# The value bias of a head attention, moved from VectorE's eviction into the matmul bank

## The reference, cut to what matters

```python
def _L1_xattn_ref(query, key, value, Wq, bq, Wk, bk, Wv, bv, Wo, bo):
    q = (query @ Wq.T + bq).reshape(b, s, N_HEADS, D_K)
    k = (key @ Wk.T + bk).reshape(b, s, N_HEADS, D_K)
    v = (value @ Wv.T + bv).reshape(b, s, N_HEADS, D_K)
    scores = jnp.einsum('bshd,bsgd->bshg', q, k) * inv_sqrt_dk
    attn = jax.nn.softmax(scores, axis=-1)
    out = jnp.einsum('bshg,bsgd->bshd', attn, v)
```

## Time and profile before

| what | value |
|---|---|
| median of 3 runs | 584.02 us (583.33 to 591.06) |
| the profiled execution's own time | 586.47 us |
| its span, first to last instruction | 584.7 us |
| mean granted TensorE clock | 0.954 of full |
| TensorE matmuls busy | 515.5 us (88%) |
| VectorE busy | 425.0 us (73%) |
| ScalarE busy | 331.8 us (57%) |
| GpSimd busy | 199.0 us (34%) |

### The profile page before, as it was taken

One profiled execution on the slowest core, in us unless ns is written; L12 is line 12 of the kernel. 1 busy time (PEld: TensorE's weight loads), 2 busy tenths in 40 slices (PEclk: granted clock), 3 DMA queues, 4 the chain that ended last, 5 costly groups with the idle time before them and its releaser, 6 DMA issues.

```text
span 584.7 us, 13038 instructions
## 1 busy us (share of the span) xinstructions
PE 515.5 (88%) x4832; PEld 321.4 (55%) x4842; DVE 425.0 (73%) x1232; ACT 331.8 (57%) x825; POOL 199.0 (34%) x309
## 2 busy tenths in 40 slices
PE   3887888999999999977488997998989989999995
PEld 2532444544455576756344556776667867655543
DVE  7878567254666667588998768753788557798996
ACT  1764435755768879655267573566566644353441
POOL 6940000024365545341345520000224221434774
PEclk9955889999999999999699999999998989999998
DMA  8700000000300000001324833000000000301101
GB/s 291 307 1 4 2 3 4 2 1 0 145 2 1 1 2 3 2 1 34 169 84 135 179 86 101 3 4 2 2 3 3 3 2 2 145 0 67 80 1 36
DMA packets 25889, 27.93 MB, mean 48 GB/s; under 512 B 18249, under 2 KB 22866, under 8 KB 24930
## 3 DMA queue, kind: packets, MB, share of 16 engines
q1 hardware_dynamic: 25826, 27.10, 14.4%
HBM read 22.14 MB, written 4.75 MB: 46 GB/s over the span
## 4 chain that ended last, share of the span: by engine, by line
PE 59%; DVE 19%; issue 8%; ACT 5%; SPq 3%; DMA 2%; POOL 2%; POOLq 0%; DVEq 0%; ACTq 0%
PE B_banks L312 4%; PE A_banks L312 4%; PE A_banks L2108 2%; PE A_banks L248 2%; PE A_banks L1014 2%; PE A_banks L1027 2%; DVE B_moe_h L2075 2%; SPq L276 2%; PE B_banks L248 2%; PE A_banks L1874 1%; DVE A_l0a_nmax L340 1%; PE B_banks L982 1%; PE A_banks L1884 1%; PE B_banks L1035 1%; PE A_banks L1035 1%
## 5 line engine op out<-in xcount | busy, mean ns | idle before, releaser
L2108 PE MATMUL A_banks<-A_moe_xT,w_moe_rows 128*128 128x512 f32 x72 | 36.0, 617 | 1.3 <-DVE A_moe_h L2075 1.3
L832 POOL TENSOR_TENSOR A_l0x_prob<-A_l0x_prob,A_l0x_inverted_sums 128x256 f32<-128x256 f32 (+1 forms) x32 | 25.9, 831 | 28.5 <-DVE A_l0x_inverted_sums L947 28.5
L2108 PE MATMUL B_banks<-B_moe_xT,w_moe_rows 128*128 128x512 f32 x72 | 34.4, 598 | 1.2 <-DVE B_moe_h L2075 1.1
L832 POOL TENSOR_TENSOR B_l0x_prob<-B_l0x_prob,B_l0x_inverted_sums 128x256 f32<-128x256 f32 (+1 forms) x32 | 25.9, 831 | 27.6 <-DVE B_l0x_inverted_sums L947 27.6
L160 POOL TENSOR_TENSOR A_l0a_rstd<-A_l0a_ve,w_const_rows 128x4 f32<-128x4 f32 x2 | 2.0, 1016 | 87.8 <-DVE A_l0a_ve L156 87.8
L379 ACT ACTIVATE A_l0a_expT<-A_banks 128x512 f32<-128x512 f32 x32 | 18.3, 603 | 18.6 <-PE A_banks L327 18.3
L849 ACT ACTIVATE B_l0x_prob<-B_l0x_prob,B_l0x_nmax 128x128 f32<-128x128 f32 x64 | 28.2, 446 | 0.9 <-DVE B_l0x_nmax L929 0.9
L849 ACT ACTIVATE A_l0x_prob<-A_l0x_prob,A_l0x_nmax 128x128 f32<-128x128 f32 x64 | 28.2, 447 | 0.0
L340 DVE TENSOR_REDUCE A_l0a_nmax<-A_banks 128x2 f32<-128x512 f32 x32 | 21.7, 687 | 8.0 <-PE A_banks L248 7.7
L379 ACT ACTIVATE B_l0a_expT<-B_banks 128x512 f32<-128x512 f32 x32 | 18.4, 600 | 15.9 <-PE B_banks L327 15.9
L340 DVE TENSOR_REDUCE B_l0a_nmax<-B_banks 128x2 f32<-128x512 f32 x32 | 21.9, 688 | 7.3 <-PE B_banks L248 7.3
(11 more groups left out here) (602 smaller groups left out, 1598.6 us busy)
## 6 DMA issues: line engine op xcount, KB each, us to landing
w_toeplitz_rows<-in_toeplitz_rows SPq DMA_DIRECT2D x1, 3072.0 KB, 13.1
w_moe_rows<-in_moe_rows SPq DMA_DIRECT2D x1, 2304.0 KB, 8.6
w_l1x_rows<-in_l1x_rows SPq DMA_DIRECT2D x1, 2048.0 KB, 8.4
A_l1x_values<-A_l1a_v_tokens SPq DMA_DIRECT2D x4, 512.0 KB, 2.6
A_l1x_v_groups<-A_l1x_values SPq DMA_DIRECT2D x16, 128.0 KB, 3.3
B_l1x_values<-B_l1a_v_tokens SPq DMA_DIRECT2D x4, 512.0 KB, 3.4
B_l1x_v_groups<-B_l1x_values SPq DMA_DIRECT2D x16, 128.0 KB, 3.3
w_l0x_vo_rows<-in_l0x_vo_rows SPq DMA_DIRECT2D x1, 1024.0 KB, 13.7
```

The lines of the kernel that those rows point to most:

```text
L832: ins = pool.tensor_tensor(pair, pair, bcast(rz[:, g % 2, i, :], 2, n), ALU.mult)
L2108: pe.matmul(hidden_bank(k)[:, :], w["moe_w3" if which else "moe_w1"][:, ORDER[i], part, :], xT[:], start=True, stop=True).then_inc(s_h.sem, 1)
```

## The change

The value bias is split once into three bfloat16 parts whose sum is the fp32 bias. GpSimd makes them, in five pieces of the program W: two casts and two subtractions of 1024 columns over 128 partitions, a memset, two copies of 32 partitions, and three memsets of one row. They lie where the spread bias lay; partitions 0 to 31 hold the high part, 32 to 63 the middle one, 64 to 95 the low one. `bias_rows` is a 96 x 128 matrix with ones in rows 0, 32 and 64. A values job becomes two products into the same bank: `bias_rows` by the parts (bfloat16, 96 rows, 512 columns), then the fp32 product as before. VectorE's sixteen additions are gone; ScalarE's `context_values` copies the bank to `vt`. TensorE waits for the parts before each lane's first job, and program W has VectorE and ScalarE wait for them before they write the buffers that GpSimd uses as scratch (`r` and `vT`). `TURNS` is new for all five engines; the GpSimd table has its five W turns right after both lanes' last piece of `rel_attention`'s preparation (L518).

```diff
--- before.py
+++ after.py
@@ -1421,6 +1421,13 @@
                 ins = act.activation(heads_kT[:, :, h], job_bank(m)[:, j * S:(j + 1) * S], ACT.Identity, bias=w["l1x_bk"][:, h:h + 1])
             ins.then_inc(s_key.sem, 1)
 
+        def context_values(m):
+            t, half = divmod(jobs[m][1], 2)
+            act.wait_ge(*s_pr(m + 1))
+            if t >= SB:
+                act.wait_ge(*s_vs(16 * (t - SB + 1)))
+            act.activation(vt[:, t % SB, half * 512:(half + 1) * 512], job_bank(m)[:, :], ACT.Copy).then_inc(s_val.sem, 1)
+
         def values(t):
             act.wait_ge(*s_rest(t + 1))
             act.activation(vals[:, t, :, 0:DV], bank[2 + t % 2][:, NQK:W].rearrange("p (h d) -> p h d", h=HK), ACT.Copy).then_inc(s_v.sem, 1)
@@ -1433,11 +1440,14 @@
             ins.then_inc(s_stk.sem, 1)
 
         def all_keys():
-            for m in range(1, JOBS, 2):
+            for m in range(JOBS):
                 yield job_time(m) + 1.0
                 if m == 1:
                     w.loaded(act, "l1x")
-                keys(m)
+                if m % 2:
+                    keys(m)
+                else:
+                    context_values(m)
 
         def all_values():
             yield 5.5
@@ -1474,14 +1484,6 @@
     def vector(dve):
         link = Chain(dve, lane)
 
-        def values(m):
-            t, half = divmod(jobs[m][1], 2)
-            dve.wait_ge(*s_pr(m + 1))
-            if t >= SB:
-                dve.wait_ge(*s_vs(16 * (t - SB + 1)))
-            dve.tensor_tensor(vt[:, t % SB, half * 512:(half + 1) * 512], job_bank(m)[:, :],
-                              w["l1x_bv"][:, half * 512:(half + 1) * 512], ALU.add).then_inc(s_val.sem, 1)
-
         def split(t, due):
             dve.wait_ge(*s_qkv(t + 1))
             if t >= 2:
@@ -1494,13 +1496,6 @@
             link.wait()
             dve.tensor_tensor(sr[:, t % 2, :], qk, hi, ALU.subtract).then_inc(s_rest.sem, 1)
 
-        def all_values():
-            for m in range(0, JOBS, 2):
-                yield job_time(m) + 1.0
-                if m == 0:
-                    w.loaded(dve, "l1x")
-                values(m)
-
         def all_splits():
             for t in range(TT):
                 yield 8.0 + 3.5 * t
@@ -1510,7 +1505,7 @@
         yield from norm.vector_stats(dve, link, x)
         yield
         norm.vector_apply(dve, xn, x, s_xn)
-        yield from interleaved([all_values(), all_splits()])
+        yield from all_splits()
         yield 26.0
         dve.wait_ge(*s_kz(2))
         dve.wait_ge(*s_stT(5))
@@ -1567,7 +1562,9 @@
                 wait_job(pe, m - 2)
             if kind == "v":
                 t, half = divmod(i, 2)
-                ins = pe.matmul(out[:, :], cT[:, t * P:(t + 1) * P], w["l1x_v"][:, half * 512:(half + 1) * 512], start=True, stop=True)
+                columns = slice(half * 512, (half + 1) * 512)
+                pe.matmul(out[:, :], w["bias_rows"], w["l1x_bv_parts"][:, columns], start=True, stop=False)
+                ins = pe.matmul(out[:, :], cT[:, t * P:(t + 1) * P], w["l1x_v"][:, columns], start=False, stop=True)
             else:
                 for j in range(2):
                     for half in range(2):
@@ -1581,6 +1578,7 @@
                 yield job_time(m)
                 if m == 0:
                     w.loaded(pe, "l1x")
+                    pe.wait_ge(*w["bias_parts"])
                 product(m)
 
         def all_projections():
@@ -2166,6 +2164,9 @@
     s_vTp, s_vT, s_vo = (st.own_sem(n) for n in ("v_transposed", "vT_ready", "product_ready"))
     st.chain = [lane.ctx.enter_context(lane.nc.semaphore("weights_chain")), 0]
     s_levels = w["levels"][0]
+    s_bv = w["bias_parts"][0]
+    high, mid = (vT[:].rearrange("p c d -> p (c d)").bitcast(BF16)[:, i * 1024:(i + 1) * 1024] for i in range(2))
+    rest = r[:].rearrange("p i d -> p (i d)")
 
     def sync(sp):
         yield 0.0
@@ -2206,6 +2207,7 @@
         link.add(dve.reciprocal(scale[:], mean[:]))
         yield
         link.wait()
+        dve.wait_ge(*w["bias_parts"])
         for i in range(2):
             link.add(dve.tensor_scalar(r[:, i, :], raw[:, i, :], scale[:, i:i + 1], MAGIC, ALU.mult, ALU.add))
             yield
@@ -2237,6 +2239,8 @@
     def scalar(act):
         for i in range(2):
             yield 61.0
+            if i == 0:
+                act.wait_ge(*w["bias_parts"])
             act.wait_ge(*s_vTp(i + 1))
             act.activation(vT[:, 4 * i:4 * i + 4, :], bank[0][:, :].rearrange("p (c d) -> p c d", c=4), ACT.Copy).then_inc(s_vT.sem, 1)
         yield 65.0
@@ -2244,7 +2248,27 @@
         act.activation(w["l0x_vo"][:], bank[0][:, 0:D], ACT.Copy, scale=1.0 / S).then_inc(s_levels, 1)
 
     def gpsimd(pool):
-        yield from ()
+
+        bias, parts, rows = w["l1x_bv"], w["l1x_bv_all_parts"], w["bias_all_rows"]
+        yield 50.0
+        w.loaded(pool, "l1x_rest")
+        pool.tensor_copy(high, bias).then_inc(s_bv, 1)
+        yield
+        pool.wait_ge(s_bv, 1)
+        pool.tensor_tensor(rest, bias, high, ALU.subtract).then_inc(s_bv, 1)
+        yield
+        pool.wait_ge(s_bv, 2)
+        pool.tensor_copy(mid, rest).then_inc(s_bv, 1)
+        yield
+        pool.wait_ge(s_bv, 3)
+        pool.tensor_tensor(parts, rest, mid, ALU.subtract).then_inc(s_bv, 1)
+        pool.memset(rows, 0.0).then_inc(s_bv, 1)
+        yield
+        pool.wait_ge(s_bv, 5)
+        pool.tensor_copy(parts[0:32, :], high[0:32, :]).then_inc(s_bv, 1)
+        pool.tensor_copy(parts[32:64, :], mid[32:64, :]).then_inc(s_bv, 1)
+        for i in (0, 32, 64):
+            pool.memset(rows[i:i + 1, :], 1.0).then_inc(s_bv, 1)
 
     return dict(tensor=tensor, vector=vector, scalar=scalar, gpsimd=gpsimd, sync=sync)
 
@@ -2390,6 +2414,10 @@
         w["context"][name] = token_tiles(dram["ctx_1024"][here])
         w["out"][name] = token_tiles(out[here])
     w["levels"] = (ctx.enter_context(nc.semaphore("weights_quantized")), 2)
+    w["bias_parts"] = (ctx.enter_context(nc.semaphore("bias_parts_ready")), 10)
+    place = w["l1x_bv"].bitcast(BF16)
+    w["l1x_bv_all_parts"], w["bias_all_rows"] = place[:, 0:1024], place[:, 1024:1024 + P]
+    w["l1x_bv_parts"], w["bias_rows"] = place[0:96, 0:1024], place[0:96, 1024:1024 + P]
     w["converted"] = (ctx.enter_context(nc.semaphore("constants_converted")), 1)
     return w, bases, half
 
@@ -2409,36 +2437,36 @@
 TURNS = {
     "tensor":
...
     "gpsimd":
-        "B1 A4 B3 A4 B1 A3 B5 A2 B1 A3 B2 A1 B3 A1 B2 A5 B2 A3 B2 A1 B1 A1 B1 A1 B1 A1 B1 A1 B1 A1 B1 A2 B1 A1 B1 A1 B2 A1 B1 A1 B1 A1 B2 A1 B2 A2 B4 A16 B16 "
...
+        "B1 A4 B3 A5 B1 A2 B4 A1 B1 A2 B1 A2 B3 A1 B2 A1 B2 W5 A5 B2 A2 B1 A1 B2 A2 B1 A1 B1 A1 B1 A1 B1 A1 B1 A2 B1 A1 B1 A1 B2 A1 B1 A1 B1 A1 B2 A1 B1 A1 B1 "
...
     "sync":
-        "W3 A1 W1 B1 W9 A1 B1 A1 B1 A1 B1 A1 B1 L2 A7 B1 A1 B2 A1 B3 A1 B3 A1 B1 A1 B1 A1 B2 A2 B2 A1 B1",
+        "W3 A1 W1 B1 W9 A1 B1 A1 B1 A1 B1 A1 B1 L2 A7 B1 A1 B3 A1 B3 A1 B2 A1 B1 A1 B2 A2 B2 A1 B1",
```

More of the change, by code:

```diff
@@ L2411 @@
     "tensor":
[8 rows of a table removed]
-    "vector":
[9 rows of a table removed]
-    "scalar":
[6 rows of a table removed]
[8 rows of a table added]
+    "vector":
[9 rows of a table added]
+    "scalar":
[6 rows of a table added]
     "gpsimd":
-        "B1 A4 B3 A4 B1 A3 B5 A2 B1 A3 B2 A1 B3 A1 B2 A5 B2 A3 B2 A1 B1 A1 B1 A1 B1 A1 B1 A1 B1 A1 B1 A2 B1 A1 B1 A1 B2 A1 B1 A1 B1 A1 B2 A1 B2 A2 B4 A16 B16 "
-        "A3 B3 A3 B1 A1 B1 A1 B1 A1 B1 A2 B2 A3 B2 A2 B2 A1 B1 A7 B1 A2 B3 A1 B2 A1 B5 A2 B4 A1 B2",
+        "B1 A4 B3 A5 B1 A2 B4 A1 B1 A2 B1 A2 B3 A1 B2 A1 B2 W5 A5 B2 A2 B1 A1 B2 A2 B1 A1 B1 A1 B1 A1 B1 A1 B1 A2 B1 A1 B1 A1 B2 A1 B1 A1 B1 A1 B2 A1 B1 A1 B1 "
+        "A1 B4 A16 B16 A3 B3 A4 B1 A1 B2 A1 B1 A2 B2 A3 B2 A1 B1 A1 B2 A8 B1 A1 B2 A2 B2 A1 B2 A1 B4 A1 B4 A1 B2",
     "sync":
-        "W3 A1 W1 B1 W9 A1 B1 A1 B1 A1 B1 A1 B1 L2 A7 B1 A1 B2 A1 B3 A1 B3 A1 B1 A1 B2 A2 B2 A1 B1",
+        "W3 A1 W1 B1 W9 A1 B1 A1 B1 A1 B1 A1 B1 L2 A7 B1 A1 B3 A1 B3 A1 B2 A1 B1 A1 B2 A2 B2 A1 B1",
 }
```

## The result

The changed kernel takes 597.76 us (median of 4 runs, 595.41 to 599.98) and the kernel before 584.2 us beside it: a ratio of 1.0263, 95% interval 1.0213 to 1.0314. It is slower by 13.6 us, not by 3.1; the forecast's range ended at 592. In what follows a ratio is taken over the fast runs of a kernel and of the kernel before alone, medians over all of its runs; where that matters, in runs two and seven, both are given.

The account below looks back on a forecast made before the run. VectorE was taken to lead from 294 to 318 us, TensorE to bound 318 to 341. 586.47 - 1.0 (copies) + 1.7 (products) - 0.3 (SyncE) + 0 (order) + 2.7 (GpSimd) = 589.6, 2.45 above the median, so 587.1; range 579.5 to 592.

Parts of the forecast that it names:

- The new order of the lanes: Jobs move between lanes, on TensorE most from 320 to 345 us: taken as 0, bound 3 us either way.
- What would make it wrong: A wait of the new orders that no single price shows, most likely between 320 and 365 us.
- Copies: ScalarE copies replace VectorE's additions, 294 to 318 us: gain 1.0 us, between 2.6 gain and 2.4 loss.
- The sign that I gave: In the profile after, the stretch of ScalarE's copies has ScalarE busy more than 22 of 24 us.
- Bias products: Sixteen on TensorE at 0.215 us; lane B's eight in the full stretch +1.7 us, lane A's covered by room.
- GpSimd's block: From about 36 us, GpSimd's long instructions hold VectorE's small steps, delaying the shifts: +2.7 us, bounds 0 and 6.7.
- SyncE: Lane B's first shift, issued at 359.64 us after its data are ready, goes earlier: gain 0.3 us, between 0 and 0.3.
- The sum without the order: The forecast of 587.1 us, slower by 3.1, in which the term for the lanes' new order was 0.
- the first (GpSimd hidden): GpSimd's work hides entirely beside VectorE's reductions or between small steps: 584.4 us, not slower; chance 0.28.
- The second: VectorE's relief is worth the chain's 2.6 us and the new order gains 3: 579.8 us, faster by 0.7%; chance 0.13.
- The third: ScalarE becomes the bound of lane B's feed-forward part: 590.8 us, slower by 1.2%; chance 0.10.
- The fourth (the clock): TensorE's half clock from 32 to 63 us becomes full, 581.6 us, or lasts longer, 592.6; chance 0.07.

Follow-up runs that it names:

- runs two: Kernel before, its sixteen additions kept, with the new turns alone up to 280 us: 594.0 us, ratio 1.0123.
- run seven: Whole change in the old turns, with GpSimd's split put late, after VectorE's weight quantization: 584.67 us, ratio 1.0001 against the kernel before.
- run one: All code of the change, with the turns of the kernel before: 587.67 us, ratio 1.0047 against the kernel before, +2.9 at equal clock.
- run eight: Of the change only ScalarE's copies for VectorE's additions, old turns, no split, no bias products: 582.66 us, ratio 0.9984 against the kernel before.
- runs five and six: Changed kernel with short fills replacing GpSimd's split, value bias left out: in the new turns 597.94 us, in the old turns 585.58 us.
- run four: Changed kernel with the old turns up to about 290 us and the new ones from there on: 588.17 us, ratio 1.0099 against the kernel before.
- Run nine: Kernel before with the new turns only from 182 to 207 us: 584.92 us, ratio 1.0021.

## Why the prediction was wrong, step by step

- **The new order of the lanes** is the step that failed. I took 0 and a bound of 3 us either way, because no row gave it a sign; it costs 11.0 us (13.9 less run one's 2.9; 11.6 by its two parts). Both the size and the symmetry were wrong. The bound was three pieces of 1.08 us. The loss is in waits of TensorE for banks in cross-attention, more than half of it (6.3 us of waits where there were 2.0), and, from 290 us on, around one stop of 2.6 us with a lower clock behind it. The trace of before pointed to the sign: TensorE is busy 67.85 of 70 us in cross-attention, so by that row no order of the same work can gain more than 2.15 us there, while each exchange can lose a wait.
- **What would make it wrong** was named rightly as a wait of the new orders, but put between 320 and 365 us, and the sum gave it nothing. Most of it lies before 240, and the late part between 310 and 345.
- **Copies**: -1.0 predicted, -1.4 measured. Reading the gaps of ScalarE against the copies worked. The sign that I gave, ScalarE busy more than 22 of 24 us, came out at 21.81 in run eight. No version gains by it: the products take back what the copies bring.
- **Bias products**: +1.7 predicted, +2.0 measured, with the lower of the two end points, 0.215 us each. If lane B's eight cost their 1.7, lane A's eight cost 0.3, nearly nothing, as assumed; no run tells the lanes apart.
- **GpSimd's block**: +2.7 predicted, +1.9 (new turns) and +2.3 (old) measured, by the mechanism named: small casts and subtractions held for a GpSimd instruction. In run one a small step sits out a subtraction, as the term had it, and a second one a copy, 2.6 us together by the lag. That L264 moved by 2.72 us in the changed kernel, the very 2.7 of the term, is luck: 2.0 of it are the split's. My durations were too long, since I scaled them by columns: a cast of 1024 takes 1.04 us, not 1.6, a subtraction 2.13, not 2.7, the whole block 9.7 and not 12.6. What the Trainium skill says in SBUF — State Buffer, "Who interferes with whom", holds here for casts (1.29 and 1.02 us) and for the subtraction with both inputs in SBUF (1.01), and for the reductions, which stay at 0.69. In run seven the steps that read a bank (0.21 to 0.23 us) aren't held either; that section's rule for two inputs in SBUF is not met by them.
- **SyncE**: the wait that the term takes away is gone. In the changed kernel lane B's first shift is copied from 372.5 to 372.8 us and issued at 372.82, while in run one, with the old turns, it is ready at 361.4 and issued at 362.68. What that brings in time can't be told from the scatter.
- **The sum without the order**, 587.1, was met by the run that is without the new order: 587.67, or +2.9 at equal clock against the 3.1 that I forecast.
- **Rivals**: the first (GpSimd hidden) is refuted by runs five and six, with the held steps in the traces. The second had the relief too high (2.6 for 1.4) and the order of the wrong sign. The third (ScalarE the bound of lane B's feed-forward part) is not what happened in the old order, where TensorE waits for no L1150; in the new one it waits 2.6 us for it, but L1150 itself comes no later: in run four lane B's starts at 308.3 us, where it started at 310.8 before, and 2.0 us of that is the lead that this run has by its clock. It is TensorE that comes to its turn too early, with nothing else in its order to do. The fourth (the clock) moves single runs by 5 us but not the difference, since the changed kernel's median clock of 0.9565 is no lower than the kernel before's; only the short stretch behind the 2.6 us stop comes with the change.

## What to carry to other kernels

When an edit comes with a new hand-made or planned order, price the order as a part of its own and on every stage, not only where the code changes; run the new code in the old order and the old code in the new order before anything is concluded about the code. Where the engine that bounds a stretch is busy 97% of it, take its idle time as the most that a new order can gain, and no such bound for the loss. By runs one and seven, long GpSimd instructions belong beside VectorE's reductions and reads of banks, not beside small steps from SBUF to SBUF.

## What the runs showed of the hardware

The granted clock differs from run to run of one kernel and goes with most of the scatter: 3.4 us for 0.01 of the mean clock. In the traces the lag between two runs of the same code is constant to 0.1 us for a hundred microseconds and more and then jumps by 1 to 4 us. Run nine shows how a difference in clock makes such a jump, with -4.5 us at 40 us from a clock of 0.99 instead of 0.80 between 20 and 40 us, in code and turns that are those of before. Two profiles alone can therefore mislead by as much as a change of 1% is worth, unless the clock is compared slice by slice. The mean clock of a run also holds what the kernel itself does to it: behind TensorE's stop of 2.6 us in run four the granted clock is 0.83 from 310 to 320 us, and 1.00 in run one. A comparison at equal clock takes such a cost out, so the lag has to be read beside it.
